# Gate of the first batch taken from the fourth batch's attention into the third's, gate-weight norms moved behind the first batch's attention

## The reference, cut to what matters

```python
# attention of the second layer: 16 heads of 16 features, context as keys and values
scores = einsum('bhqd,bhkd->bhqk', qw, kw) * inv_sqrt_d
ctx = einsum('bhqk,bhkd->bhqd', softmax(scores), vw)
x = x + ctx @ Wo + bo
# second mixture: the input is layernorm(x); its gate picks one expert of eight for a token
x_red = h @ w_red                                               # (tokens, 16)
wg_n = wg / maximum(norm(wg, axis=1, keepdims=True), 0.0001)    # (8, 16)
logits = x_red @ wg_n.T
scores = max(softmax(logits)); idx = argmax(softmax(logits))
o = (gelu(h @ W1[idx] + b1[idx]) @ W2[idx] + b2[idx]) * scores
x = x + o
```

## Time and profile before

| | us |
|---|---|
| median of 3 runs (range) | 1082.23 (1081.29 to 1084.33) |
| the profiled execution | 1093.17 |
| its span, first to last instruction | 1091.1 |
| first stage, attend(0): 668 to 730 | 62 |
| second stage, attend(1): 730 to 791 | 61 |
| third stage, attend(2): 791 to 854 | 63 |
| fourth stage, attend(3): 854 to 953 | 99 |

### The profile page before, as it was taken

The page is one execution under the profiler, slowest core; times in us unless marked ns, Lnnn a source line. Parts: engine busy times, 40 slices in busy tenths (PEclk is TensorE's granted clock), DMA queues, the critical chain, the costliest instruction groups (busy, mean ns, idle before and its releaser), DMA issues.

```text
span 1091.1 us, 19956 instructions
## 1 busy us (share of the span) xinstructions
PE 951.9 (87%) x6592; PEld 586.3 (54%) x6592; DVE 725.4 (66%) x1959; ACT 459.0 (42%) x1022; POOL 222.4 (20%) x198
## 2 busy tenths in 40 slices
PE   5989998998987999999998678889899787877785
PEld 3656666574754887888854433234343242345564
DVE  5473868578798666666644676687848776464676
ACT  4354543234225443444423203576646456622222
POOL 0313320101112443443210010100100011113453
PEclk9989999898988999999999956999959797788998
DMA  8541020026183111111126861722611036243231
GB/s 298 182 164 69 1 78 0 20 59 174 59 288 108 50 46 55 46 51 50 44 96 159 150 141 23 120 37 62 108 28 40 21 84 170 78 155 89 81 102 33
DMA packets 70239, 98.63 MB, mean 90 GB/s; under 512 B 8796, under 2 KB 57183, under 8 KB 67712
## 3 DMA queue, kind: packets, MB, share of 16 engines
q1 hardware_dynamic: 60000, 61.67, 20.7%
q0 software_dynamic: 10144, 35.69, 12.0%
HBM read 71.04 MB, written 27.15 MB: 90 GB/s over the span
## 4 chain that ended last, share of the span: by engine, by line
PE 61%; DVE 22%; ACT 6%; DMA 4%; issue 3%; another core or an unknown queue 2%; SPq 0%; ACTq 0%; POOLq 0%; DVEq 0%
PE pb L1050 11%; PE pb L1070 7%; PE pb L1162 4%; PE pb L883 4%; PE pb L1071 4%; PE pb L1186 3%; PE pb L1140 3%; PE pb L836 3%; PE pb L872 3%; PE pb L892 3%; PE pb L813 3%; PE pb L849 3%; DVE MX L2051 2%; PE pb L807 2%; ACT EX L1477 2%
## 5 line engine op out<-in xcount | busy, mean ns | idle before, releaser
L2051 DVE TENSOR_REDUCE MX<-pb 128x1 f32<-128x512 f32 x256 | 160.5, 683 | 47.0 <-PE pb L1140 45.7
L1415 ACT ACTIVATE m<-pb,b1m 128x128 f32<-128x128 f32 x404 | 114.9, 369 | 173.4 <-PE pb L1050 143.6
L1477 ACT ACTIVATE EX<-pb 128x512 f32<-128x512 f32 x256 | 137.0, 600 | 105.4 <-PE pb L1186 104.1
L1050 PE MATMUL pb<-xt,w1h 128*128 128x128 f16 x1616 | 157.3, 221 | 5.9 <-issue 3.8
L1070 PE MATMUL pb<-w,mh 128*128 x404 | 150.0, 381 | 10.1 <-DVE ml L1948 9.5
L1050 PEld LDWEIGHTS pb<-xt,w1h 128*128 x1616 | 120.4, 99 | 43.7 <-issue 8.3
L1050 PE MATMUL pb<-xt,w1l 128*128 128x128 f16 x808 | 113.2, 221 | 1.4 <-issue 1.3
L1071 PE MATMUL pb<-w,ml 128*128 x404 | 110.4, 273 | 0.4 <-issue 0.4
L807 PE MATMUL pb<-identh 128*128 128x512 f16 x373 | 96.7, 413 | 15.3 <-DVE identh L1585 7.4
L1186 PE MATMUL pb<-QS,KS 49*128 49x512 f32 x256 | 80.3, 505 | 13.3 <-ACT EX L1477 8.8
L1140 PE MATMUL pb<-KS,QS 48*128 48x512 f32 x256 | 71.4, 531 | 12.2 <-DVE MX L2051 8.0
(11 more groups left out here) (320 smaller groups left out, 1536.3 us busy)
## 6 DMA issues: line engine op xcount, KB each, us to landing
SR<-in_w1m SPq DMA_DIRECT2D x20, 512.0 KB, 5.4
SR<-in_w2m SPq DMA_DIRECT2D x12, 512.0 KB, 5.1
KS<-kd SPq DMA_DIRECT2D x48, 128.0 KB, 6.7
QS<-qd POOLq DMA_DIRECT2D x18, 256.0 KB, 9.1
kd<-KHL POOLq DMA_DIRECT2D x8, 512.0 KB, 5.7
vd<-VAB POOLq DMA_DIRECT2D x4, 1024.0 KB, 4.3
rows<-HL POOLq DMA_DIRECT2D x8, 512.0 KB, 3.9
GB<-outs SPq DMA_DIRECT2D x8, 512.0 KB, 7.5
```

The costliest lines, as they stand in the source:

```text
L1050: ins = pe.matmul(k.ap[:, h4 * TOK:(h4 + 1) * TOK], wt[:, bass.ds(regs[j], 128)], M.xt[j % 2][:, xc, :], start=i == 0, stop=i == 5)
L1415: ins = act.activation(M.m32[x % 2][:, h4, :], k.ap[:, h4 * TOK:(h4 + 1) * TOK], M.func, bias=M.b1[:, bass.ds(reg + 4 * g + h4, 1)], scale ...
L1477: act.activation(EX[m % len(EX)][:, i, :], k.ap, ACT.Exp, scale=0.25).then_inc(k.out, 1)
L2051: v.tensor_reduce(mx[:, t, 2 * s + j:2 * s + j + 1], k.ap, AX.X, ALU.max).then_inc(k.out, 1)
```

## The change

`wg_norm` is called ahead of attend(1) in place of ahead of attend(3). `gate(0)` leaves the side `early` of attend(3) and stands at the end of `side` of attend(2), behind the tail of batch 1 and the load of the values of batch 3. The memset of `R1.Mc` goes from `wg_norm` into `gate(0)`, because that tile lies in the query buffer that attend(1) still reads. Nothing is computed more or less.

```diff
             for b in range(NB):
                 last = b + 1 == NB
-                if last:
+                if b == 1:
                     p["wg_norm"]()
                 side = chain(tails[b - 1] if b else nothing(), p["load_v"](b + 1) if 1 <= b < NB - 1 else nothing(),
                              p["qprep"](b + 2) if b + 2 < NB else nothing(),
-                             chain(p["split"]("n"), islice(down, 1), pause(6), islice(down, 4), pause(4), islice(down, 4)) if last else nothing())
-                early = gates(range(NB - 1)) if last else nothing()
+                             chain(p["split"]("n"), islice(down, 1), pause(6), islice(down, 4), pause(4), islice(down, 4)) if last else nothing(),
+                             gates([0]) if b == NB - 2 else nothing())
+                early = gates(range(1, NB - 1)) if last else nothing()
                 beside(p["attend"](b, tails), (ms, 66 / 64), (side, 1.0), (early, 1.1), drain=False)
...
             def wg_norm():
-                v.memset(R1.Mc[:, :], 0.0)
                 v.memset(scr[:, :, :], 0.0)
...
                 w.wait_ge(*k.mm)
+                if b == 0:
+                    v.memset(R1.Mc[:, :], 0.0)
                 v.tensor_copy(lgz1[:, 4 * b:4 * b + 4, :], k.ap[:, 0:4 * E].rearrange("p (t e) -> p t e", e=E)).then_inc(k.out, 1)
```

## The result

| | before | changed |
|---|---|---|
| median us (runs) | 1083.28 (4) | 1103.14 (4: 1095.17 to 1109.0) |
| ratio, with its interval | | 1.0172 [1.0117, 1.0227] |
| profiled execution, span, mean clock | 1093.17, 1091.1, 0.911 | 1101.42, 1099.4, 0.907 |

What follows compares the result with a forecast made beforehand. The prediction took PE to bound all four stages. Its terms, 4.5 + 4 + 8.7 - 3.5 + 2.5 - 13, gave +3.2 us on the median 1082.23, so 1085.4 us, range 1076 to 1095.

Steps and rivals of the forecast that it cites:

- Term 3: Gate 0 in stage three: 6.5 us of PE work at full clock plus a 2.2 us wait beside the layernorm, +8.7.
- half clock only at stage two: Half clock was priced behind the norms' wait ahead of stage two, +4 us, and not behind gate 0 in stage three.
- term 2: Half clock behind the norms' wait at the start of stage two: +4 us, bounds 0 and 11.4.
- rival A: Clock holds behind the norms' wait and PSUM banks cover gate 0's layernorm: faster, 1077 to 1079 us; chance 0.25.
- Terms 1 and 2: Start of stage two: PE waits for the norms, +4.5 us, then half clock behind that wait, +4 us.
- Term 4: Start of stage four without the norms: layernorm, fills and all behind them come earlier, -3.5 us, bounds -2.5 to -5.
- term 5: Stage four's first two gate places: 8 more fills there, 1.9 to 3.7 us, taken as +2.5.
- term 6: End of stage four without a third gate: PE work and two waits go, -13 us, bounds -9 to -13.7.
- B: Half clock spreads from the stall at stage two (1093 us) or PE's waits at stage three's gate (1089); chance 0.17.
- C: Gate 0's stores delay batch 3's maxima, so stage four begins with a 2.1 us wait: 1088 us; chance 0.08.

Runs made afterwards that it cites:

- e1: Changed kernel with gate 0 back in stage four, only the norms ahead of stage two; ratio 1.0029 to the kernel before, median 1072.1 us.
- a1: The changed kernel itself, run once more beside the follow-up kernels; ratio 1.0196 to the kernel before, median 1083.5 us.
- e6: Changed kernel with all of gate 0 begun at the start of stage three, where DVE is idle; ratio 1.0035 to the kernel before, median 1066.8 us.
- e12: Changed kernel with the norms in stage one and all early gates in stage four; ratio 1.0020 to the kernel before, median 1071.9 us.
- e10: e1 with DVE's layernorm of batch 0 computed once more, for nothing, at gate 0's changed place in stage three; ratio 1.0105 to the kernel before.
- x1: e8 with gate 0 stopped ahead of its logits in stage three and finished in stage four; ratio 0.9910 to the kernel before, median 1070.2 us.
- x3: e8 with gate 0's ranks, placing and DVE's chain for these moved to stage four; ratio 1.0013 to the kernel before, median 1073.1 us.
- e14: e12 with DVE's layernorm of gate 0 alone moved into DVE's gap at the start of stage three; ratio 0.9987 to the kernel before, median 1065.1 us.
- e2: Changed kernel with the norms ahead of stage three in place of stage two; ratio 1.0111 to the kernel before, median 1079.0 us.
- e3: Changed kernel with each gate's DVE layernorm cut into three pieces, attention steps between them; ratio 1.0114 to the kernel before, median 1081.6 us.
- e9: Changed kernel with six more fills on PE ahead of gate 0's ranks in stage three; ratio 1.0116 to the kernel before, median 1075.7 us.
- e8: Changed kernel with only DVE's layernorm of gate 0 moved to the start of stage three; ratio 0.9993 to the kernel before, median 1079.1 us.

## Why the prediction was wrong, by its steps

**Term 3 failed (gate 0 in stage three, +8.7, bounds 6.5 to 12).** Of the 18.9 us between e1 and a1 in stage three, PE's work at full clock is some 6 (60.2 - 54.2, the busy time of the stage in e6 and e1, which both have 10 us of half clock), against 6.5 in the term. This part was right. Idle time of PE grew by 5.1 (10.7 against 5.6) where I took 2.2. The rest of a1's busy time, 7.9 us, is half clock, for which the term had nothing. In the first profile, against before, the same sum is 5.2 of idle and 16.7 of busy time, 6 of it work and 10 to 11 half clock.

The 2.2 was read from a place that is not like this one. In the earlier trace rows the layernorm comes right behind the norms. PE had already stood 4.54 us there, and beside the layernorm it still had 4.4 us of queued matmuls to do at half clock (858.83 to 863.2). Only the end of the layernorm was left to wait for. In e12, without the norms ahead, the same matmuls run at full clock and are done at 855.9, 0.9 us behind the layernorm's start, and the wait is 5.37 us, not 2.18. In stage three it was 4.92 and 4.90. So the right value lay near my upper bound for the wait, 5.5.

The step "half clock only at stage two" failed with it. I priced the clock behind the wait at L1230 (term 2) and left the same term out behind a wait of the same kind in stage three. e10 shows it: 13 us at half clock behind 4.90 us of waiting for DVE. Behind the 4.9 us of waiting in the changed kernel it was 6 us, about 3 us lost. The larger loss, the second stretch, I did not foresee; the earlier trace rows showed the ranks only as 0.6 us of work. It moved when they were moved (x1, x3); why it comes there and not at other places of theirs isn't shown.

The Trainium skill, "TensorE: Matmul & The Clock Gate", section "Loop structure matters more than you think", says that a read-out of PSUM by DVE does not break the warmth of PE, in a loop nest whose next matmuls follow at once. That can't be carried over to a read-out that PE has to wait for, as rival A has it: here waits for DVE of 4.90 and 5.37 us came with 0.50 behind them, and with 0.31 in place of 5.37 the clock stayed at 1.00.

**Terms 1 and 2 (+8.5):** +6.5 in the changed kernel, +6.4 in e1. The wait was 4.53 (4.5 forecast); the clock was at half for 7 us, of which PE worked through 5, +1.9 where I took +4.

**Term 4 (-3.5):** e12 has stage four 3.7 us shorter than before (102.4 against 106.1) without the norms. From the end of the matmuls ahead of the norms' place to the fills it is 11.1 us before and 7.5 in e12, as the forecast had it (11 and 7). But the 3.6 us are made otherwise. The waits went from 4.54 + 2.18 to 5.37, which gives 1.4, and the other 2.3 are the matmuls in between, which no longer stand behind a wait and run at full clock. The size is right, in part by luck. In the changed kernel the wait at this place was 3.76 us, and in a1 5.38.

**Terms 5 and 6 (-10.5):** -9.7 together (102.6 in e1, 92.9 in a1): +2.2 up to the round-20 transposes, where term 5 gave +2.5, and -11.9 behind them, where term 6 gave -13. Right.

**Rivals.** B was nearest. It names "PE's waits at the gate in stage three" as an opener of half clock, but gave 4 us to it, so its 1089 was far too low. C did not happen: `QS<-md` was issued 1.5 us behind batch 3's `md<-MTR` (864.08 and 865.54). A's condition held to the letter (1.00 from 735 on), but L1230 ended its wait at 730.13, 5 us earlier than I had set it, and half clock had stood until then. The kernel was slower all the same, since A too took term 3 as small.

## What to carry to other kernels

Work moved into a stage that two engines share must be priced on the engine that has just now no slack. In this kernel a serial chain of 5.5 us on DVE cost PE 3.8 to 5.4 us of waiting wherever DVE was behind. In a gap of DVE in the same stage it cost 1.1 us of waiting (e6), or 0.1 us of stage length (e14). A wait measured right behind another wait is too small a price, because PE still had work of its own to catch up on there. And where PE waits some 5 us, add the half clock that may follow: here 3.4 to 14 us of it, which costs up to half its length in a stage that PE bounds (6.3 us in e10, some 3 in the changed kernel).

## What the runs showed of the hardware

The clock moves this kernel's time as much as any edit here. The kernel before ran from 1054 us at 0.932 to 1088 at 0.891 with nothing changed. Splitting the wait of 4.9 us into 0.7, 2.1 and 1.3 did not spare the fall to half clock, and in a1 the clock fell at the ranks with no wait over 0.6 us in the 13 us before. The stretches behind the ranks were 34 and 17 us long in two profiles of the changed kernel itself, and 17, 10, 10 and 27 in e2, e3, e9 and e8, so a single profile doesn't give their price. The end of the program, from stage four's last group on, took 135 to 136 us in the first comparison and 118 to 121 in all experiments, on both of their chips, for the same work. PE's clock there was no lower in the first comparison (0.90 and 0.93, against 0.91 in a1 and e1); what it is that differs was not looked into.
